# Selective-scan block and mixture of experts: gates re-tiled, three-part second layers for eight pairs of every batch

## The reference

```python
x = x + ssm(ctx, z=layernorm(x))     # in_proj, conv of 4 taps, silu u, B/C/dt projections,
                                     # delta = softplus(.), state scan over 16 states, + D*u, * silu(z)
h = layernorm(x)
shared = sum(relu(h @ sw1[i] + sb1[i]) @ sw2[i] + sb2[i] for i in range(2)) / 2
g = softmax top-6 of (h @ router_w + router_b), renormalized, 0 elsewhere      # 32 experts
routed = sum(g[:, e] * (relu(h @ rw1[e] + rb1[e]) @ rw2[e] + rb2[e]) for e in range(32))
x = x + shared + routed              # hidden width of an expert: 176
```

## Time and profile before

| | us |
|---|---|
| median of 3 runs | 404.87 (403.12 to 405.67) |
| the profiled execution, its own time | 406.21 |
| its span, first to last instruction | 404.4 |
| TensorE busy in the span | 360.7 (89%) |
| VectorE, ScalarE, GpSimd busy | 259.2, 216.2, 197.3 |
| moved by DMA | 75.45 MB, 187 GB/s |

### The profile page before, as it was taken

How to read it: one execution, slowest core, us unless ns; L and a number is a source line. 1 busy time by engine, 2 the same in 40 slices (tenths; PEclk the granted TensorE clock), 3 DMA queues, 4 the chain that set the end, 5 groups by cost and what they waited for, 6 DMA issues and landing times.

```text
span 404.4 us, 6983 instructions
## 1 busy us (share of the span) xinstructions
PE 360.7 (89%) x2255; PEld 319.4 (79%) x2255; DVE 259.2 (64%) x443; ACT 216.2 (53%) x542; POOL 197.3 (49%) x152
## 2 busy tenths in 40 slices
PE   4448678857999899999999899999999999999996
PEld 2225346746998788998988788989999989999996
DVE  3269995737975954769947646699775534444453
ACT  2757736618745335538634327477532436567662
POOL 0499760578974300259847002389761023354542
PEclk9857999996999999999999999999999999999999
DMA  7487760295999613688899323877995237777520
GB/s 241 117 298 227 189 190 28 94 301 158 273 218 271 215 54 76 179 278 237 262 261 244 114 61 113 300 237 241 260 268 168 72 107 241 219 234 182 154 58 26
DMA packets 46752, 75.45 MB, mean 187 GB/s; under 512 B 6754, under 2 KB 16388, under 8 KB 46724
## 3 DMA queue, kind: packets, MB, share of 16 engines
q1 hardware_dynamic: 46724, 75.11, 64.0%
HBM read 73.77 MB, written 1.31 MB: 186 GB/s over the span
## 4 chain that ended last, share of the span: by engine, by line
PE 52%; DVE 18%; DMA 10%; issue 7%; SPq 5%; ACT 4%; POOL 2%; DVEq 1%; ACTq 0%; POOLq 0%
PE acc L532 24%; DVE dA L747 8%; PE z L551 7%; PE z L552 7%; PE z L553 7%; DMA gone<-gates 6%; SPq L366 2%; DMA bt<-bc 2%; DMA grem<-in_w 2%; DVE cv L722 2%; DVE hg L841 2%; DVE pr L758 2%; PE z L463 1%; SPq L361 1%; POOL bu L895 1%
## 5 line engine op out<-in xcount | busy, mean ns | idle before, releaser
L532 PE MATMUL acc<-hg,w 128*128 128x256 f32 x564 | 135.8, 384 | 8.5 <-DVE hg L841 7.1
L895 POOL TENSOR_TENSOR bu<-bt,du 128x512 f32<-128x512 f32 x64 | 81.1, 1278 | 102.1 <-DVE du L741 53.5
L679 ACT ACTIVATE z<-z,par 128x256 f32<-128x256 f32 x188 | 75.7, 439 | 92.7 <-PE z L553 92.5
L532 PEld LDWEIGHTS acc<-hg,w 128*128 128x128 f32 x564 | 103.3, 192 | 21.5 <-DVE hg L841 8.2
L551 PE MATMUL z<-xh,w1l 128*128 128x256 f32 (+1 forms) x376 | 118.8, 316 | 0.0
L553 PE MATMUL z<-xh,w1h 128*128 128x256 f32 (+1 forms) x376 | 106.2, 283 | 0.0
L552 PE MATMUL z<-xl,w1h 128*128 128x256 f32 (+1 forms) x376 | 106.0, 282 | 0.0
L747 DVE TENSOR_TENSOR_SCAN dA<-dA,bu 128x512 f32<-128x512 f32 x64 | 78.2, 1222 | 7.6 <-POOL bu L895 7.1
L841 DVE TENSOR_TENSOR hg<-z,gone 128x512 f32<-128x512 f32 x64 | 44.0, 687 | 56.3 <-ACT z L679 36.3
L551 PEld LDWEIGHTS z<-xh,w1l 128*128 128x128 f32 x376 | 71.4, 190 | 5.2 <-issue 3.3
L552 PEld LDWEIGHTS z<-xl,w1h 128*128 128x128 f32 x376 | 70.9, 189 | 1.6
(11 more groups left out here) (101 smaller groups left out, 359.2 us busy)
## 6 DMA issues: line engine op xcount, KB each, us to landing
w<-in_w SPq DMA_DIRECT2D x92, 256.0 KB, 5.0
gone<-gates SPq DMA_DIRECT2D x64, 256.0 KB, 5.3
bt<-bc SPq DMA_DIRECT2D x32, 256.0 KB, 5.6
ct<-bc SPq DMA_DIRECT2D x32, 256.0 KB, 6.2
grem<-in_w SPq DMA_DIRECT2D x11, 512.0 KB, 6.3
grem<-gates SPq DMA_DIRECT2D x96, 48.0 KB, 4.8
xr<-in_xr SPq DMA_DIRECT2D x4, 256.0 KB, 6.8
x<-in_xT SPq DMA_DIRECT2D x4, 256.0 KB, 5.0
```

The lines of the kernel that those rows point to most:

```text
L532: mm = pe.matmul(acc[:, k, :], weights, h, start=t + k + n == 0, stop=last, skip_group_check=True)
L679: ins = act.activation(z[p % ZB][:, i, :], z[p % ZB][:, i, :], ACT.Relu, bias=b1[:, t:t + 1])
L895: pool.tensor_tensor(bu[:, r, :].rearrange("p (j l) -> p j l", j=2), bt[:, c % BRING], du[:, k:k + 1, :].broadcast_to([P, 2, L]), ALU.mult ...
```

## The change

The order of the routed hidden units becomes: two groups of 16 experts; in a group, 11 parts of 16 units; for each part two tiles of eight experts by 16 units. Every pair of a group of 11 (pairs 2 to 12, 13 to 23) then needs the same two gate tiles, and four tiles `gt` (8 gate rows, each on 16 partitions) serve the batch. They are loaded by four transfers of 128 KB, in two halves. `gone`, `grem` and their waits are gone. The staging ring gets a fourth slot, shares memory with `w2h`, `w2l` and `gt`, and all `w1` loads now stand before the first gates; the `w1h`/`w1l` steps move accordingly (11 and 10 of them in `HEAD`). `v` of the softplus, `y` and `xc` go to the PSUM tiles `dA`, the square of `xc` moves from DVE to a step `sq` on ACT. Pairs 16 to 23 are split in every batch; outside the last batch their `hl` is made by POOL.

```diff
-WRING = 3
+WRING = 4
-BACK = [..., ("centre", 19), ("var", 20), ...
+BACK = [..., ("centre", 19), ("sq", 19), ("var", 20), ...
-HEAD += [("taps", 1), ("w1h", 0), ("w1l", 0), ("econv", 1), (("sum", NC - 1), 0), (("warm", None, 14), 0), ("x1", 0),
+HEAD += [("taps", 1), ("w1h", 0), ("w1l", 0), ("econv", 1), (("sum", NC - 1), 0), ("w1h", 0), ("w1l", 0), (("warm", None, 14), 0),
...
-SPLIT = []
+SPLIT = [16, 17, 18, 19, 20, 21, 22, 23]
-        xc, xs, sq = ya[:, :, 0:L], ya[:, :, L:2 * L], y
+        xs, sq = ya[:, :, L:2 * L], y
-        xdt = dA[0]
+        xdt, xc = dA
+            def load_gates(b, half):
+                for g in (2 * half, 2 * half + 1):
+                    eng.dma_start(gt[:, g, :], gates_d[b % 2, g * GEXP:(g + 1) * GEXP, :].rearrange(
+                        "(e o) l -> e o l", o=1).broadcast_to([GEXP, GROW, L])).then_inc(ld_g[half], 16)
-            load_w1(8)
-            load_w1(9)
+            for i in range(8, NW):
+                load_w1(i)
             spill_bc(1)
...
+                eng.wait_ge(S["spilled"], 16 * b + 16)
+                if b:
+                    eng.wait_ge(S["hg_done"], (b - 1) * NP + SINGLE0 + NPART)
+                load_gates(b, 0)
                 if b:
                     eng.wait_ge(S["hg_done"], b * NP)
-                for p in range(SINGLE0, SINGLE0 + GRING):
-                    gate_one(b, p)
+                load_gates(b, 1)
...
             def second_layer(b, p):
                 if split(b, p):
-                    pe.wait_ge(S["hl_done"], nth_split(b, p))
+                    if last(b):
+                        pe.wait_ge(S["hl_done"], p + 1)
+                    else:
+                        pe.wait_ge(S["pool_hl_done"], nth_split(b, p))
...
-                        act.activation(v[:, k, :], xdt[:, k, :], ACT.Relu, bias=dtb[:, k:k + 1])
+                        act.activation(xdt[:, k, :], xdt[:, k, :], ACT.Relu, bias=dtb[:, k:k + 1])
+                elif name == "sq":
+                    act.wait_ge(S["xc_done"], b + 1)
+                    act.activation(sq, xc[:], ACT.Square).then_inc(S["sq_done"], 1)
-                    bk.then(dve.tensor_tensor(y, y, sz[:], ALU.mult))
-                    dve.tensor_tensor(x1[:, b % 2], y, x1[:, b % 2], ALU.add).then_inc(S["x1_done"], 1)
+                    bk.then(dve.tensor_tensor(xc[:], xc[:], sz[:], ALU.mult))
+                    dve.tensor_tensor(x1[:, b % 2], xc[:], x1[:, b % 2], ALU.add).then_inc(S["x1_done"], 1)
+                    half = (p - SINGLE0) // NPART
+                    dve.wait_ge(ld_g[half], (b + 1) * 32)
+                    ins = dve.tensor_tensor(hg[:, p % 4], z[p % ZB][:], gt[:, 2 * half:2 * half + 2, :], ALU.mult)
...
             def pair(b, p, beside):          # GpSimd, behind its steps and w2l of the slot
+                if not (type(b) is int and b == 0 and p == 0):
+                    d, q = before(b, p, 1)
+                    if q in SPLIT and not last(d):
+                        n = len(PAIRS[q])
+                        pool.wait_ge(S["hh_done"], nth_split(d, q))
+                        pool.tensor_tensor(hl[:, q % SKEW, 0:n], hg[:, q % 4, 0:n], hh[:, q % SKEW, 0:n].bitcast(F32),
+                                           ALU.subtract).then_inc(S["pool_hl_done"], 1)
```

More of the change, by code:

```diff
@@ L52 @@
 ZB = 4
-GRING = 4
 SKEW = 3
@@ L68 @@
 ZGATE = [("stats", 2), ("rs1", 3), ("nb1", 4), ("zz", 5), ("ez1", 6), ("ez2", 7), ("ez3", 8), ("zmul", 10)]
-BACK = [("yfold", 16), ("x1", 17), ("mean", 18), ("centre", 19), ("var", 20), ("r2", 20), ("norm", 20), ("logits", 21),
+BACK = [("yfold", 16), ("x1", 17), ("mean", 18), ("centre", 19), ("sq", 19), ("var", 20), ("r2", 20), ("norm", 20), ("logits", 21),
         ("xh", 21), ("xl", 21), ("top", 21), ("ex", 22), ("gates", 22), ("turn", 23)]
@@ L99 @@
     HEAD += [(("sum", _c - 1), 0)] if _c else []
-HEAD += [("taps", 1), ("w1h", 0), ("w1l", 0), ("econv", 1), (("sum", NC - 1), 0), (("warm", None, 14), 0), ("x1", 0),
-         (("warm", "conv_done", 14), 1), ("mean", 0), (("warm", None, 8), 0), ("uclip", 1), ("usig", 1), ("w1h", 0), ("centre", 0),
-         ("u", 1), ("var", 0), ("r2", 0), ("w1h", 0), ("xall", 1), (("warm", None, 4), 0), ("dtl", 1), ("norm", 0), ("dt", 1),
-         (("warm", None, 6), 0), ("xh", 0), ("logits", 0), ("xl", 0), ("sp", 1), ("top", 0), ("ex", 0), ("delta", 1)]
+HEAD += [("taps", 1), ("w1h", 0), ("w1l", 0), ("econv", 1), (("sum", NC - 1), 0), ("w1h", 0), ("w1l", 0), (("warm", None, 14), 0),
+         ("x1", 0), (("warm", "conv_done", 14), 1), ("mean", 0), (("warm", None, 8), 0), ("uclip", 1), ("usig", 1), ("w1h", 0),
+         ("w1l", 0), ("centre", 0), ("sq", 0), ("u", 1), ("var", 0), ("r2", 0), ("w1h", 0), ("xall", 1), (("warm", None, 4), 0),
+         ("dtl", 1), ("norm", 0), ("dt", 1), (("warm", None, 6), 0), ("xh", 0), ("logits", 0), ("xl", 0), ("sp", 1), ("top", 0),
+         ("ex", 0), ("delta", 1)]
 OPEN = [[("gates", 0), (("bu", 0, 0), 1), (("bu", 0, 1), 1)],
@@ L106 @@
                           ("prod", 0, 1))],
[L107 to L111 removed]
+        [("turn", 0)] + [(n, 1) for n in (("bu", 1, 1), ("decay", 1, 0), ("decay", 1, 1), ("scan", 1, 0), ("prod", 1, 0),
+                                          ("fold", 1, 0), "stats", "w1h", "w1l")]]
+SPLIT = [16, 17, 18, 19, 20, 21, 22, 23]
 BIG = 2.0 ** 63
@@ L302, in nth_split, with last @@
             return b * len(SPLIT) + sum(split(b, q) for q in range(p + 1))
+        def last(b):
+            return type(b) is int and b == B - 1
         def first(b):
@@ L844, in pair @@
                 ins.then_inc(S["hg_done"], 1)
-                if exists(b, p, 1) and split(*before(b, p, 1)):
-                    lower_h(*before(b, p, 1))
+                if last(b) and p:
+                    lower_h(b, p - 1)
                 if p == SKEW - 1 and exists(b, p, SKEW):
```

88 lines of the change are left out of this document (27 added, 61 removed).

## The result

The changed kernel takes 401.76 us (median of 11 runs, 400.50 to 405.69), the kernel before 406.80 in the runs beside it (11 runs, 403.12 to 409.53). The ratio is 0.990, 95% interval 0.986 to 0.994: faster by about 1%, some 4 to 5 us, where 14 were forecast. The forecast was 390.8 with a range of 386 to 399, so the time lies outside it. Part of that is the base: the forecast stood beside three runs of before with a median of 404.87. Beside the 406.80 measured here the same saving of 14 would give 392.8, and the time is still 9 above it.

The account below looks back on a forecast made before the run. Taken as TensorE-bound, with stretches where others make it wait. Terms -8.1, -0.7, -0.8, -1.25, -1.6 and -1.6 sum to -14.05 us: 392.2 for the profiled execution, 390.8 beside the median, range 386 to 399.

Parts of the forecast that it names:

- the end of batch 2: Batch 2 from slot 16 on: split slots save 2.3 us after new waits, meetings cost 0.7, together -1.6.
- the head: Before pair 0: `sq` queues on ACT behind a `w1h`, +0.5 us; the extra casts fall in idle stretches, 0.
- the w1 stall: Batch 0, pairs 3 to 7: with early `w1` loads pair 7 opens 8.1 us sooner, the head's +0.5 included.
- sign of the lock: PE waits of over 2 us before `logits` would show the forecast wrong through DVE and POOL locking.
- The gate loads: Fewer gate transfers end waits of `hg` and late `w2` loads: -0.8 us in batch 1 before slot 16.
- the walk: Slots 16 to 2 of the next batch, step by step: 2.3 us of new waits against 2.4 saved, old waits gone.
- Pair 14 and the clock: Batch 0: 0.5 us from the lowered clock after the idle and 0.2 at pair 14, together -0.7.
- The split slots: Pairs 16 to 23, batches 0 to 2: each slot 0.30 us shorter, 2.4 a batch, 7.2 if others keep up.
- The meetings in batch 2: DVE steps with two SBUF inputs wait for POOL in batch 2: +0.7 us, only `norm` and `du` lacking slack.
- The lock decides: Rival: in slots 16 to 23 every two-operand DVE step waits 1.3 us for POOL; 412.4 us, chance 0.05.
- ACT is the queue: Rival: in slots 16 to 23 ACT's queue makes two chains lose 1.3 us more each per batch; 397.3, chance 0.2.
- The stall is only exchanged: Rival: first gates or `bt` hold DVE at pair 2 or 3 instead, 8 us stay; 398.9, chance 0.1.

Follow-up runs that it names:

- after_again: The changed kernel run once more with no edit: 401.94 us, ratio 0.989 to the kernel before.
- g4: g2 with the last two pieces of `w1` loaded behind the first gates, as before the change: 398.75 us, ratio 0.978.
- g2: f1 with the head's `w1h` and `w1l` casts where they stood before the change: 391.97 us, ratio 0.961.
- e1: The changed kernel with the head's weight casts where they stood before the change: 401.87 us, ratio 0.989.
- f1: The changed kernel with only pairs 16 to 19 split in batches 0 to 2, four instead of eight: 392.81 us, ratio 0.964.
- e2: The changed kernel with no split pairs in batches 0 to 2: 397.17 us, ratio 0.977.
- e8: The changed kernel with POOL waiting, in pair 22 of batches 0 to 2, for DVE's gates step before its `w2l`: 397.11 us, ratio 0.971.

## Why the prediction was wrong, step by step

The spans of before and after_again differ by 4.0 where 14.05 were forecast. Three terms hold the missing 10: the end of batch 2 (+3.7 for -1.6), the head (+3.8 for +0.5) and the w1 stall (-7.0 for -8.6). Of the signs that the forecast named, batch 1 came out right (83.1 for 83.5), batches 0 and 2 did not (83.5 for 81, 82.3 for 78.5). Its sign of the lock, a wait of over 2 us before `logits`, looked at the wrong step: that wait was 0.78 in batch 2 and none elsewhere, and the long one stood before `turn`.

- **The w1 stall: right, a little large.** From pair 0 to pair 7 the time fell from 27.2 to 20.0 and 20.2, by 7.0 to 7.2, and by 6.8 in g4 against g2. The forecast had 8.1 with 0.5 of head inside, so 8.6. PE still waits 0.6 to 0.8 and 0.2 for DVE's `hg` in slots 5 and 6.
- **The head, +0.5: failed.** The step was "one more `w1h` and two more `w1l` lie in the head, in stretches where ACT and POOL idle: 0". They cost POOL nothing. But a DVE step that lies beside one waits it out: 1.7 at `uclip`, and then `usig` and a `w1h` in front of `sq`. From the last scan to `var` that is 2.1 us; the rest of the 3.8 lies within the scatter of the scans in front, and 3.6 more came with the lower clock in after. e1 shows the meeting by taking it away (1.7 of the 2.1). It does not show that time is to be had there: what e1 won, `mean` gave back to DVE's scan, and g2 against f1 is no more than a hint.
- **The gate loads: right.** -0.8 was forecast for batch 1 before slot 16, and -0.9 came. The waits of the earlier trace rows are gone; e2 measures 2.6 and 2.9 for the two later stretches, where the walk had 0.3 + 2.0 and 0.59 + 1.82 + 0.24.
- **Pair 14 and the clock: right.** -0.7 was forecast, and -0.8 stands from 0/7 to 0/15: 0.5 in the slot of pair 7, which had been at the lower clock, and 0.3 in that of pair 14.
- **The split slots: price right, number of usable slots wrong.** 0.30 a slot holds in the main: f1 gets 0.9 for four, 0.23 each. The totals were near for batch 1 (its stretch fell by 2.0 for a forecast of 1.6) and off by 0.45 for batch 0 (-0.8 for -1.25), but not for the reasons given. Of the waits walked, `dt` came (0.51 for 0.6) and so did `hl`(23) in slot 2 (0.6 for 0.9); the 0.1 before `var` and the 0.7 in slot 1 did not. `turn` waited instead. In batch 0, behind the wait for `dt`, the slot of pair 22 also ran at the lower clock (4.46 against 2.96 in batch 1).
- **The meetings in batch 2, +0.7: here the forecast failed most.** The stretch was to fall by 1.6 and grew by 3.7. The step was "only `norm` and `du` do not" have slack, with 0.7 for batch 2. The mechanism was named and the earlier trace rows held: the later of the two instructions waits for the end of the earlier. The list of DVE's steps that can meet POOL was wrong. It held the passes of 512 columns (`x1`, `u`, `norm`, `xl`, `du`) and left out the gates step, whose `mask`, `em` and `g` are a few tenths of a us. But the price is the length of POOL's instruction, not of DVE's: these three paid 1.0, 1.0 and 1.9 in batch 2, more than the 3.1 that the forecast had for all meetings in three batches. The counted `norm` paid too, through its step with one input (1.26 for 0.29), and gave the 0.78 before `logits`. In batches 0 and 1 `mask` and `em` paid the same, but `w2h` of pair 23 stands behind `sp` on ACT, so POOL's last two products come after `g`. Batch 2 has no `sp`; the walk took it for the easy batch for that reason, and it was the worst. e8 shows the cause there by experiment. For the 1.9 and 1.0 that the split costs in batches 0 and 1 (after_again less e2) no run parts the meetings from ACT's queue and the clock.
- **The rivals.** "The lock decides" had this mechanism, with 19 meetings of 1.3 on the path; what came was fewer meetings on the path: the gates step in every batch, `norm` in batch 2, and `uclip` in the head. "ACT is the queue" was nearer in time (397.3), but e8, with ACT's list unchanged, refutes it for the end of batch 2; elsewhere ACT held PE for 0.51 before `dt` in batches 0 and 1. "The stall is only exchanged" is refuted by the second column of the table.

The Trainium skill (SBUF — State Buffer, "Who interferes with whom") also lists `tensor_scalar` among the operations that can take the shared ports in a mode for which a single SBUF input is enough. The trace agrees: `uclip` 0.42 and 2.15 beside `w1l`, the two `g` 0.39 and 2.28, the one-input step of `norm` 0.29 and 1.26. The forecast had used the page for instructions with two inputs only.

One correction to the description of the change: the larger staging ring of `w1` shares its memory with `w2l` and `w2h`, not with the gate tiles.

## What to carry to other kernels

Before work is given to an idle GpSimd, list every VectorE instruction beside it that has two SBUF inputs or is a `tensor_scalar`, however small, and price each meeting at up to one whole GpSimd instruction. A chain of small steps in front of a matmul is the dearest place: end GpSimd's work before such a chain (f1) or make it wait for the chain's end (e8, one added wait: 1.8% of the time, 4.3 us of it in that stretch). And a stretch that one engine alone binds has no slack: every new wait shows there in full (the 3.13 before `turn`), and with TensorE the clock may follow it down (1.4 more in the next pair).

## What the runs showed of the hardware

- A `tensor_scalar` with one input from SBUF waits for a running GpSimd instruction (2.15 for 0.42), while `hg`, which has one of its two inputs in PSUM, took 0.67 to 0.69 beside a running GpSimd instruction and alone.
- The same idle of 2.76 before `var` was followed by 10 us and more at the lower clock in after and by full clock up to pair 0 in after_again, while the idle of 3.13 in batch 2 was followed by 3.4 us of it in both. What decides it in the head stays open; it moves this kernel's time by 3.6 us.
- A wait on TensorE can be paid twice. Of the 3.7 at the end of batch 2, 1.4 are pair 0 of batch 3 at the lower clock.
